# Causal attention in one Trainium2 kernel: a lead of four maximum units in place of ten, caught up over the first six steps

## The reference, cut to what matters

```
score = jnp.einsum('bnqd,bnkd->bnqk', Q, K) / jnp.sqrt(jnp.float32(D_K))
causal = jnp.triu(jnp.ones((s, s), dtype=bool), k=1)
score = jnp.where(causal[None, None], -jnp.inf, score)
attn = jax.nn.softmax(score, axis=-1)
out = jnp.einsum('bnqk,bnkd->bnqd', attn, V)
```

## Time and profile before

| | us |
|---|---|
| median of 3 runs | 1476.43 |
| lowest and highest | 1474.38 and 1478.0 |
| the profiled execution, its own time | 1478.0 |
| its span in the trace | 1476.2 |
| mean granted clock of TensorE | 0.954 |
| busy: TensorE, VectorE, ScalarE | 1264.9, 1129.2, 1121.5 |

### The profile page before, as it was taken

The page is one execution under the profiler, slowest core; times in us unless marked ns, Lnnn a source line. Parts: engine busy times, 40 slices in busy tenths (PEclk is TensorE's granted clock), DMA queues, the critical chain, the costliest instruction groups (busy, mean ns, idle before and its releaser), DMA issues.

```text
span 1476.2 us, 22855 instructions
## 1 busy us (share of the span) xinstructions
PE 1264.9 (86%) x8290; PEld 655.0 (44%) x8290; DVE 1129.2 (76%) x2049; ACT 1121.5 (76%) x1604; POOL 351.2 (24%) x434
## 2 busy tenths in 40 slices
PE   6699999895788788888888898988999988888996
PEld 3344444362111111111111146666777766566874
DVE  8888987456787978877758778597766686777898
ACT  4178877756999999999999945654576567778885
POOL 2500001642000000001100037553546548340000
PEclk9599999997799999999999999999999999999998
DMA  6300110003100000100000030023333233011111
GB/s 193 116 24 24 35 36 4 2 1 111 47 22 1 22 22 1 38 1 22 22 0 1 1 151 1 1 62 92 101 94 109 77 117 121 29 36 29 43 45 57
DMA packets 41088, 70.50 MB, mean 48 GB/s; under 512 B 6416, under 2 KB 14864, under 8 KB 40208
## 3 DMA queue, kind: packets, MB, share of 16 engines
q1 hardware_dynamic: 40976, 69.05, 15.0%
HBM read 59.26 MB, written 9.76 MB: 47 GB/s over the span
## 4 chain that ended last, share of the span: by engine, by line
PE 33%; DVE 26%; ACT 20%; issue 13%; POOL 4%; DMA 1%; SPq 1%; POOLq 0%; ACTq 0%; DVEq 0%
ACT SHARED L1140 12%; DVE SHARED L1176 8%; PE PS L823 5%; PE PS L787 3%; DVE PS L2350 2%; PE PS L2140 2%; PE PS L645 2%; PE PS L2142 2%; PE PS L2141 2%; PE PS L1366 2%; PE PS L712 2%; PE PS L2149 2%; PE PS L2146 1%; PE PS L2147 1%; DVE X L284 1%
## 5 line engine op out<-in xcount | busy, mean ns | idle before, releaser
L1140 ACT ACTIVATE SHARED<-PS 128x1536 f32<-128x1536 f32 (+1 forms) x346 | 457.6, 1450 | 15.9 <-PE PS L1036 10.0
L1176 DVE TENSOR_TENSOR SHARED<-SHARED 128x1536 f32<-128x1536 f32 (+1 forms) x170 | 276.6, 1704 | 34.7 <-ACT SHARED L1140 34.7
L1036 PE MATMUL PS<-QS,KS 48*128 48x512 bf16 (+1 forms) x1006 | 208.6, 398 | 84.7 <-ACT SHARED L1140 77.2
L803 ACT ACTIVATE SHARED<-PS 128x512 f32<-128x512 f32 (+3 forms) x384 | 163.6, 493 | 72.6 <-PE PS L791 64.1
L1036 PEld LDWEIGHTS PS<-QS,KS 48*128 48x128 bf16 (+1 forms) x1006 | 38.5, 95 | 298.7 <-ACT SHARED L1140 269.2
L2140 PE MATMUL PS<-ROUNDED 128*128 128x512 f32 x328 | 139.1, 424 | 15.6 <-DVE ROUNDED L2337 9.2
L1049 PE MATMUL PS<-SHARED,Vg 128*16 128x512 f32 x1024 | 137.1, 609 | 4.7 <-DVE SHARED L1176 4.3
L732 DVE TENSOR_REDUCE NM<-PS 128x2 f32<-128x1024 f32 (+3 forms) x128 | 124.1, 1020 | 13.0 <-PE PS L718 12.3
L2142 PE MATMUL PS<-ROUNDED 128*128 128x512 f32 x328 | 130.8, 399 | 0.0
L2141 PE MATMUL PS<-ROUNDED 128*128 128x512 f32 x328 | 130.6, 398 | 0.0
L2270 ACT ACTIVATE ROUNDED<-PS 128x512 fp32r<-128x512 f32 x100 | 59.8, 598 | 91.3 <-DVE PS L2350 89.6
(11 more groups left out here) (279 smaller groups left out, 2473.4 us busy)
## 6 DMA issues: line engine op xcount, KB each, us to landing
SHARED<-wx SPq DMA_DIRECT2D x64, 256.0 KB, 3.1
SHARED<-in_moe SPq DMA_DIRECT2D x3, 1600.0 KB, 11.1
SHARED<-wx SPq DMA_DIRECT2D x16, 224.0 KB, 2.9
SHARED<-kx SPq DMA_DIRECT2D x32, 96.0 KB
KS<-kx SPq DMA_DIRECT2D x32, 96.0 KB
SHARED<-wx SPq DMA_DIRECT2D x16, 192.0 KB, 2.8
SHARED<-wx SPq DMA_DIRECT2D x16, 160.0 KB, 2.7
qx<-SHARED SPq DMA_DIRECT2D x16, 128.0 KB, 2.4
```

What stands on the lines that cost most here:

```text
L803: act.activation(PB[t % 3][:, h, q0:CH], bank(RING0[n % 3], q0), ACT.Exp, scale=SCORE_SCALE)\
L1036: ins = pe.matmul(bank((v % 2) * GRP + f - a), KS[g % 2][r, h // 2, kt * P:kt * P + P], QS[g % 2][r, h // 2, qh * CH:(qh + 1) * CH], start ...
L1140: act.activation(dst, PS[:, (v % 2) * GRP * CH:((v % 2) * GRP + b - a) * CH], ACT.Exp if second == qh else ACT.Sigmoid, scale=SCORE_SCALE)\
L1176: dve.tensor_tensor(ex_tile(j), ex_tile(j), GR[w % RING][:, 0:(b - a) * CH], ALU.mult)\
```

## The change

LEAD goes from 10 to 4. A function `ahead(t)` says how many units stand before step t: 28 before step 0, then three in each of the steps 0 to 5, and two in each step from there. Before step 6 both kernels have done 46 units, and from there on their orders are the same. In a step with three units one stands after the first pair of scores and two after the second.

```
-        LEAD = 10
+        LEAD = 4
+        CATCH_UP = 6
+
+        def ahead(t):
+
+            return NMAX + LEAD + 2 * t + min(t, CATCH_UP)
...
-            for m in range(NMAX + LEAD):
+            for m in range(ahead(0)):
                 unit(m)
             for g in range(NG):
                 for s in range(NSTEP):
                     t = NSTEP * g + s
-                    m = NMAX * (g + 1) + LEAD + 2 * s
+                    m = ahead(t)
...
                     pe_scores(pe, g, s, 1)
-                    unit(m + 1)
+                    for k in range(m + 1, ahead(t + 1)):
+                        unit(k)
                     if t:
                         pe_weighted(pe, t - 1, 1)
...
-            for m in range(NMAX + LEAD):
+            for m in range(ahead(0)):
                 unit(m)
             for g in range(NG):
                 for s in range(NSTEP):
-                    m = NMAX * (g + 1) + LEAD + 2 * s
-                    unit(m)
-                    unit(m + 1)
+                    for m in range(ahead(NSTEP * g + s), ahead(NSTEP * g + s + 1)):
+                        unit(m)
```

## The result

The changed kernel takes 1481.02 us, the median of 20 runs, against 1475.56 us for the kernel before in 20 runs beside them. The ratio is 1.0035, with a 95% interval from 1.0028 to 1.0042: 5.2 us slower, between 4.1 and 6.2. The forecast was 1480.4 with a range from 1476.6 to 1483.4. The median lies in the range and 0.6 us from the forecast. The 5.2 us are just on the side of "slower by over 0.3%" (4.4 us), which had the chance 0.40 and not the larger one, and the interval reaches down to 4.1 us.

The account below looks back on a forecast made before the run. VectorE bounds up to the first score, TensorE after it. Reduce 46 was put at 93.4 (90.7 + 2.7 idle), unit 46 +4.0 us late; the median 1476.43 + 4.0 gives 1480.4, range 1476.6 to 1483.4.

Parts of the forecast that it names:

- The first score waits for the rows: Start of group 0: without six units ahead, the score waits for the rows of maxima; start 0.6 us earlier.
- I take 72.2, as read in this group: Landing of group 0's rows of maxima, taken from the old trace at 72.2, with bounds 70.8 and 72.2.
- The estimate from the Trainium skill: Round trip of the rows from a fixed DMA cost of about 2.0 us: landing about 70.9, sum +2.7.
- The delay is 1.65 us plus VectorE's idle time: Reduce 46, step 6: 73.4 plus 17.3 us of reduces gives 90.7 against 89.05, plus idle time in steps 0 to 5.
- The idle time of 2.7 us: VectorE's gaps in steps 0 to 5, summed as 0.5 + 1.15 + 1.0 us.
- The walk: Step-by-step count of VectorE's gaps: step 0 0.5, step 1 1.15, step 2 none, steps 3 to 5 1.0 us.
- I take the same moment: TensorE's clock was assumed to reach 1.00 at about 80.4, as in the kernel before, despite waits of 0.3 to 0.8 us.
- The rival with the late rise: Clock stays at 0.50 beyond 80.4, over steps 3 and 4: +5 to +6, 1481.4 to 1482.4; chance 0.20.
- The upper bound of 3.1 us: Most VectorE could idle in steps 0 to 5: the old kernel's 3.1 us, with three reduces per step instead of two.
- the prediction's own signs: Signs of wrong: score by 71, rise not at 80.4, copies nearing old times, VectorE idle in steps 0 to 5 not near 2.7.
- The delay stays: From step 6 on: orders alike, TensorE the bound, groups 26.74 us apart, so the +4.0 us is not regained.
- The rival that took TensorE to have room: Idle time and slack take up the catch-up, or later groups work it off: -0.6, 1475.8; chance 0.10.

Follow-up runs that it names:

- fill_steps: Changed kernel plus unread extra matmuls behind units 12 to 27, 14 ahead of the first score, two in each of steps 1, 2, 4, 5: 1.0024 of before.
- fill_after: Changed kernel plus unread extra matmuls behind units 12 to 27 and 14 more while TensorE waits for the rows of maxima: 1.0035 of before.
- light: Changed kernel with reduces 28 to 33 reading only 128 keys per head instead of 384 or 512: 0.9991 of before.
- lead8: Kernel with LEAD 8 and CATCH_UP 2, against the changed kernel's 4 and 6: 1.0018 of before.
- lead6: Kernel with LEAD 6 and CATCH_UP 4, against the changed kernel's 4 and 6: 1.0034 of before.
- fill_before: Kernel before plus one unread extra matmul behind each of units 12 to 33 of 256 keys or more: 1.0009 of before.
- light_before: Kernel before with reduces 28 to 33 reading only 128 keys per head instead of 384 or 512: 0.9986 of before.
- fill3_before: Kernel before plus unread extra matmuls of 512 to 1024 columns, spread behind units 12 to 33 to fit under the reduces: 1.0006 of before.
- slow_catch: Changed kernel with the catch-up spread over twelve steps, a third unit in every second step only: 1.0031 of before.
- fill2_before: Kernel before plus unread 512-column matmuls, one behind units 12 to 21 of 256 keys or more, two behind each of 22 to 33: 0.9996 of before.
- keep4: Changed kernel with CATCH_UP 0, the lead of four never caught up in any group: 1513.47 against 1477.41 us, one run.

## Why the prediction held, and where it did not

**The first score waits for the rows: right.** TensorE waited 3.92 us for the transfer, and the bottleneck ahead of the score moved from VectorE to the round trip.

**When the rows land: wrong by 1.6 us.** The forecast took 72.2 from the trace and named 70.8 as the other bound. It was 70.6, with a write of 1.72 us instead of 3.67. The start won 2.0 us (4.6 against 6.7 from the write), not 0.6. The step that failed is "I take 72.2, as read in this group": it took the 3.67 us of the write over from the kernel before. The estimate from the Trainium skill (DMA: Bandwidth & Descriptors, the two cost components) had landed at 70.9, nearer than the row taken from this group, though the page gives that cost for transfers issued by GpSimd and these are SyncE's; its conclusion of +2.7 us was farther off, because of the next points.

**The delay is 1.65 us plus VectorE's idle time: the form held, the work was 0.5 us short.** With the landing as it was the fixed part is nothing: 71.8 + 17.3 = 89.1 against 89.05. The changed trace has 22.0 us between reduces 28 and 46. Of these 4.1 are gaps, so the reduces took 17.9 us and not 17.3. The kernel before shows the same: 89.05 - 68.24 = 20.8 us with 3.1 of gaps leave 17.7.

**The idle time of 2.7 us: undersized by 1.4.** The walk gave steps 0 and 1 gaps of 0.5 and 1.15 us, and they were 0.41 and 1.14. It gave steps 3 to 5 1.0 us, and they had 1.04, 0.63, 0.52 and 0.40, 2.6 us. The step that failed is "I take the same moment" for the rise of the clock at 80.4. It rose at 89.7, and steps 3 to 5 ran at the low clock. With the clock held full in fill_steps these steps had 1.3 us of gaps, near the 1.0 of the walk; in fill_after, where the clock fell at 80.7, they had 3.1. No kernel here has this order with a rise at 80.4 itself. The rival with the late rise named this mechanism and gave it 0.20; its "a rise at 87 or later adds 1 to 2 us" fits the 1.3 to 1.6 found. The upper bound of 3.1 us was also wrong: "there are now three reduces in a step to cover them" did not hold at the low clock. Why the rise came late is argued only: the units of the changed kernel waited for reduces ahead of 80.4 and those of the kernel before hardly did. In light the clock rose at 77.0 with TensorE busy for 5.97 of the 6.4 us from 70.6 on, and in the changed kernel it did not with 6.08 of the same 6.4 us.

**The errors cancel, and that is luck.** 1.6 us too late a start stand against 0.5 us too little work and 1.4 to 1.5 too little idle time. They leave 4.4 to 4.6 against the forecast of 4.0, and 5.2 in the times. The number was right for a mixture of the forecast and two of its rivals. By the prediction's own signs it was wrong in three of four: the first score came before 71, the clock rose at another moment than 80.4, and the idle time wasn't near 2.7 us. A smaller slip had no weight: the formula gives 1.65 + 2.7 = 4.35 us for reduce 46, and the sum went by unit 46 with 4.0; measured they were 4.7 and 4.5.

**The delay stays: right.** The pace behind group 0 is 26.73 us against 26.74. The rival that took TensorE to have room, by the share of weight loading (11.2 of 26.8 us), has fallen: in the changed kernel no group behind the first regains anything, and the copies stay 4.4 us late up to the last group. TensorE's matmuls were busy for 25.3 of 26.7 us, and that share fits the lack of room.

**The chances.** The bound of 0.3% was 4.4 us and the outcome 5.2. Looking back, the late rise should have had more than 0.20: the prediction itself counted waits of 0.3 to 0.8 us for TensorE where it had hardly any before.

What stays open is how the delay divides. Behind the first score the changed kernel loses 6.6 us and the start gives 2.0 back. Of the 6.6, 3.6 stay when VectorE is light, and 0.9 at least go away with a full clock; the rest lies between the waits of the two engines for each other and the clock, and every means of holding the clock up costs TensorE time.

## What to carry to other kernels

In this kernel a lead of work ahead of a latency had to be as long as that latency in the bound engine's time; of the leads 4, 6, 8 and 10 the longest was the fastest, and none beyond ten was tried. Six reduces, 6.3 us, filled a round trip of 4.6 to 6 us, and taking them out won 2.0 us at the start and cost 6.6 us behind it. When work is moved from under a wait to a place where two engines already take turns, count each engine's sum and then add waits of both. And where a change puts waits into TensorE's stretch, write down what happens if the clock rises late, and price the forecast for it rather than only a rival.

## What the runs showed of the hardware

**A write of 16 KB to DRAM took 1.7 us to 3.7 us, and the longest times came with an instruction fetch in the same stretch.** The DMA view from the write's issue to the first read, first of before, then of after (queue, packets, MB, share; the last line has KB and us to landing):

```profile
q8 instruction: 1, 0.02, 2.4%
q1 hardware_dynamic: 80, 0.02, 2.2%
...
mx<-MT SPq DMA_DIRECT2D x1, 16.0 KB, 3.6
```

```profile
q1 hardware_dynamic: 80, 0.02, 3.9%
...
mx<-MT SPq DMA_DIRECT2D x1, 16.0 KB, 1.7
```

In group 0 the 13 kernels fall in two sets: with an instruction packet in that stretch the reads could be issued 3.67, 3.54, 3.29, 2.24, 2.41, 2.36, 3.63 and 2.47 us after the write (before, lead8, lead6, fill_before, fill_after, fill_steps, light_before, fill3_before), without one 1.72, 1.74, 1.73, 1.83 and 1.73 us (changed, light, slow_catch, fill2_before, keep4). The unfilled kernels with a lead of four, whose TensorE has issued fewer instructions by then, are all among the latter, and so is fill2_before with its lead of ten. That TensorE's place in its program sets when the packet comes wasn't tried by itself. Nor is the fetch the whole of it. The rows of group 1 in the changed kernel:

```profile
97.50 0.50 SPq L774 DMA_DIRECT2D mx<-MT  x1
99.94 1.23 SPq L778 DMA_DIRECT2D SHARED<-mx  x2
```

No instruction packet lies between these two, and the write took 2.44 us (2.30 in the kernel before, also without one). In groups 2 to 7 of the two kernels it took 2.09 to 2.59 us with a packet, and 2.31, 1.74 and 1.74 without.

**Where TensorE's clock rose or fell could not be read from its busy time.** It fell from 1.00 to 0.50 in fill_after behind a stretch with 5.78 of 7.50 us busy, and stayed at 1.00 in fill_steps behind one with 5.75 of 7.50. It did not rise in fill_before in 14 us without a gap, up to 80.4, and did at 67.7 and 70.7 in the two denser fillings. What in them made the difference was not tried apart.
